# One tile's fp16 parts ahead of a normalisation, one weight's bound and split a group sooner, three products among the last contexts

## The reference

```python
xn = _layernorm(x, axis=-1)
q, k, v = (proj(Wq), proj(Wk), proj(Wv))            # xn @ W.T, 16 heads of 32
scores = einsum('bhqd,bhkd->bhqk', q, k) / sqrt(32)  # causal
ctx = einsum('bhqk,bhkd->bhqd', softmax(scores), v)
s = ctx @ Wo.T
hidden = fwht(silu(xn @ W1.T) * (xn @ W3.T))
out = x + s * silu(hidden @ W2.T)
```

## Time and profile before

| | us |
|---|---|
| median of 3 runs | 944.32 |
| lowest, highest | 943.84, 944.62 |
| the profiled execution | 944.66 |
| its span, first to last instruction | 943.0 |
| PE busy in the span | 928.3 (98%) |
| DVE, ACT, POOL busy | 728.0, 625.5, 339.0 |

### The profile page before, as it was taken

One profiled execution on the slowest core, in us unless ns is written; L12 is line 12 of the kernel. 1 busy time (PEld: TensorE's weight loads), 2 busy tenths in 40 slices (PEclk: granted clock), 3 DMA queues, 4 the chain that ended last, 5 costly groups with the idle time before them and its releaser, 6 DMA issues. The chain is left out here.

```text
span 943.0 us, 19017 instructions
## 1 busy us (share of the span) xinstructions
PE 928.3 (98%) x6500; PEld 566.6 (60%) x6500; DVE 728.0 (77%) x1416; ACT 625.5 (66%) x1340; POOL 339.0 (36%) x591
## 2 busy tenths in 40 slices
PE   8999999999999999999999999999999999999997
PEld 7764566666666656744468656566665666575443
DVE  7886998998998988846665579989898899833343
ACT  4456889989889877833344358787887888833221
POOL 1896664665665442000000114344344353410000
PEclk9999999999999999999999999999999999999999
DMA  9797245544343414661236622323323232150111
GB/s 291 270 252 228 80 114 151 143 118 118 86 121 90 118 31 124 221 226 44 67 103 244 201 57 80 91 58 95 76 75 92 61 81 58 46 202 22 45 45 45
DMA packets 57920, 110.09 MB, mean 117 GB/s; under 512 B 5600, under 2 KB 22624, under 8 KB 57312
## 3 DMA queue, kind: packets, MB, share of 16 engines
q1 hardware_dynamic: 57824, 108.88, 38.9%
HBM read 79.23 MB, written 29.36 MB: 115 GB/s over the span
## 5 line engine op out<-in xcount | busy, mean ns | idle before, releaser
L1264 DVE TENSOR_TENSOR p_lo<-stages,p_hi 128x512 f16<-128x512 f32 (+2 forms) x288 | 201.7, 710 | 25.3 <-ACT p_hi L878 23.7
L1613 PE MATMUL f<-x_hi,w_lo 128*128 128x512 f16 x512 | 195.6, 382 | 0.0
L1613 PE MATMUL f<-x_lo,w_hi 128*128 128x512 f16 x512 | 194.8, 380 | 0.0
L1613 PE MATMUL f<-x_hi,w_hi 128*128 128x512 f16 x512 | 194.5, 380 | 0.0
L868 ACT ACTIVATE stages<-s 128x512 f32<-128x512 f32 (+2 forms) x288 | 150.6, 524 | 57.9 <-PE s L1573 55.5
L878 ACT ACTIVATE p_hi<-stages 128x512 f16<-128x512 f32 (+2 forms) x288 | 160.5, 557 | 25.6 <-POOL stages L699 16.4
L1573 PE MATMUL s<-qk_st 98*128 98x512 f32 (+2 forms) x384 | 129.9, 416 | 1.7 <-DMA qk_st<-m_lo 1.5
L699 POOL TENSOR_SCALAR_AFFINE_SELECT stages<-stages 128x128 f32<-128x128 f32 x192 | 61.4, 325 | 167.9 <-ACT stages L868 167.4
L707 POOL TENSOR_TENSOR w_lo<-w,w_hi 128x256 f16<-128x256 f32 x128 | 95.5, 775 | 55.2 <-ACT w_hi L931 52.8
L1251 DVE CUSTOM_DVE_ANT_0 m<-m,causal 128x1024 f32<-128x1024 f32 (+1 forms) x98 | 104.5, 1066 | 3.8 <-PE m L1554 2.7
L986 ACT ACTIVATE h_hi<-hidden 128x1024 f16<-128x1024 f32 x32 | 33.8, 1057 | 97.1 <-PE f L1411 97.1
(11 more groups left out here) (224 smaller groups left out, 1907.9 us busy)
## 6 DMA issues: line engine op xcount, KB each, us to landing
qk_st<-qk_parts SPq DMA_DIRECT2D x96, 256.0 KB, 4.3
w<-w1w SPq DMA_DIRECT2D x32, 512.0 KB, 3.6
qk_parts<-qk_hi SPq DMA_DIRECT2D x32, 256.0 KB, 3.5
qk_parts<-qk_lo SPq DMA_DIRECT2D x32, 256.0 KB, 4.4
scan<-w1w SPq DMA_DIRECT2D x12, 512.0 KB, 5.6
wht_in<-w SPq DMA_DIRECT2D x4, 1024.0 KB, 10.6
w_butterflied<-wht_in SPq DMA_DIRECT2D x4, 1024.0 KB, 5.7
x_in<-x SPq DMA_DIRECT2D x16, 256.0 KB, 2.9
```

The costliest lines, as they stand in the source:

```text
L1264: dve.tensor_tensor(p_lo[s][:], expd[q % NE][:, 0:end - need], p_hi[s][:], ALU.subtract).then_inc(p_lo_done, 1)
L1613: mm = pe.matmul(F[m][:, 0, :], w, v, start=k == 0, stop=k == GMM - 1)
```

## The change

Three edits. In the projection of batch 0 the fp16 parts of tile 0 (`x16(b, 0)`) come ahead of the second normalisation, on ACT (the square root) and on DVE. The steps of Wv are each one group sooner: absolute values after groups 4 and 5, the bound after group 8, scaling after groups 9 and 10, splitting after groups 11 and 12 on DVE. (The scaling and splitting also in batch 1.) And in slot 194 the last three products of the network stand directly ahead of context 191.

```diff
-WV_ABS_AFTER = {5: (0, 1), 6: (2, 3)}
-BOUND_AFTER = 9
-WV_AT = {10: (0, 1), 11: (2, 3)}
+WV_ABS_AFTER = {4: (0, 1), 5: (2, 3)}
+BOUND_AFTER = 8
+WV_AT = {9: (0, 1), 10: (2, 3)}
+LAST_FFN = 3
...
@@ ACT, project
-                    if b == 0 and g == ROOT_AFTER:
-                        root(b, 1)
                     for t in XT_AFTER.get(g, ()):
                         xt(b, t)
...
                     for t in X16_AFTER.get(g, ()):
                         x16(b, t)
+                    if b == 0 and g == ROOT_AFTER:
+                        root(b, 1)
...
@@ DVE, project
-                    if b == 0 and g == ROOT_AFTER:
-                        normalise(b, 1)
                     for t in XT_AFTER.get(g, ()):
                         xt(b, t)
                     for t in X16_AFTER.get(g, ()):
                         x16(b, t)
                     if b == 0:
+                        if g == ROOT_AFTER:
+                            normalise(b, 1)
...
@@ PE, heads
                     kept = 1 if (g in CTX_PLAN or b == 0 and g in MAX_PLAN) and g < SLOTS else 0
+                    if g == SLOTS + 2:
+                        kept = LAST_FFN
                     some_ffn(at, ffn_upto(g) - kept)
...
                         for q in range(first, end):
+                            if q == SLOTS - 1:
+                                some_ffn(ffn_upto(g) - kept, ffn_upto(g))
                             context(n0 * NS + q)
...
-                    some_ffn(ffn_upto(g) - kept, ffn_upto(g))
+                    if g < SLOTS:
+                        some_ffn(ffn_upto(g) - kept, ffn_upto(g))
```

## The result

| | before | after |
|---|---|---|
| median, us | 944.43 (10 runs) | 948.93 (10 runs) |
| ratio, 95% interval | | 1.0047 (1.0034 to 1.0061) |
| the profiled execution, us | 944.66 | 950.89 |
| its span, us | 943.0 | 949.2 |
| TensorE busy in the span, us | 928.3 | 930.6 |

The change makes the kernel 4.5 us slower. The forecast was +1.7 (946.0, range 944.9 to 947.6), so the sign is right and the size is not. The ten executions after the change read like this, time and mean granted clock: 945.74 (0.999), 946.13 (0.999), 947.68 (0.996), 947.70 (0.998), 948.30 (0.995), 949.57 (0.996), 949.75 (0.996), 950.50 (0.996), 950.89 (0.995), 951.12 (0.995). The two in which the clock stayed at 0.999 took what was forecast.

A forecast was written before the change was run, and what follows sets the result against it. TensorE was taken as the bound, busy 928.3 of 943.0 us. Group 8 +2.58, V0 -0.91 and the rest 0 gave +1.7 us, so 946.0 against the median, with an 8-in-10 range of 944.9 to 947.6.

The forecast's parts named there:

- Tile 0's fp16 parts: Before tile 4's transpose: the 0.82 us wait goes, normalisation comes 0.60 later; the gain is worth nothing inside group 8's wait.
- The absolute values: Ahead of tile 7's lo part: four VectorE steps, in turns with GpSimd's additions, start group 8 2.58 us later.
- The tie at the third absolute value: VectorE and GpSimd start together there; VectorE was taken as served first, its step taking 0.68 us instead of 1.78.
- The slack of 0.27 us before group 8: Before the change, tile 7's lo part ended at 36.91 and group 8, which waits for it, started at 37.18.
- The bound, the split and V0: At the projection's end: with the Wv steps a group sooner, V0's wait goes, 0.91 us back.
- The last three products: End of each batch's heads: the wait only moves from context 191 to 190; worth 0, from -0.1 to +0.1 us.
- The clock: Rival: TensorE's clock falls to half in the wait before group 8, costing 1.5 us, 947.5; chance 0.10.
- The tie served to GpSimd: Rival: GpSimd goes first at the third absolute value, adding 1.10 us, 947.1; chance 0.20.
- "Faster": Rival: absolute values take plain 0.60 us slots without turns, group 8 starts at 37.0, 943.2 us; chance 0.07.

The follow-up runs named there:

- the run that priced it: Changed kernel with the absolute values on ScalarE, plus seven extra repeats of tile 7's lo part on VectorE: 949.20 us, 1.0059 to the kernel before.
- The kernel kept busy: Changed kernel with 24 extra identity transposes on TensorE ahead of its wait before group 8: 947.57 us, 1.0035 to the kernel before.
- the later slab load: Changed kernel with the 1 MB load of W2's second slab issued after group 1's stores: 946.21 us, 1.0022 to the kernel before.

## Why the prediction was wrong, step by step

- **Tile 0's fp16 parts: right.** The wait before tile 4 is gone, the normalisation and GpSimd's first addition are 0.60 later (GpSimd 27.59 against 26.46, where group 2's lo part, ahead of them, was already 0.53 later at 22.72), and the gain disappears in the wait before group 8. Alone it brings no gain that can be told.
- **The absolute values: the mechanism right, the size off.** From the end of `x16_lo(3)` to the end of `xt_lo(7)` the forecast had 39.64 - 31.39 = 8.25 us, the trace has 41.51 - 32.98 = 8.53. The tie at the third absolute value went to VectorE (0.68 us), as chosen, which is partly luck: in one of four traces it went the other way. The first was longer than thought (1.56 us; 32.64 - 31.39 = 1.25 in the forecast). What failed is the start of that chain. The prediction took 31.39 from the trace of before as a fixed time. It hangs on the landing of group 0's stores, which is no fixed time, and that trace had the earliest. The queue began 1.59 later, as ScalarE's step did (29.95 against 28.35), while TensorE was only 0.97 later by its start; the difference, 0.62, and the 0.28 of the chain are in the wait, which became 4.38 us instead of 3.5. The slack of 0.27 us before group 8 was of that trace as well: the trace of the last products alone, with the same order there, has 0.91 us of wait.
- **The bound, the split and V0: right.** V0 starts without a wait.
- **The last three products: right**, 1.0001 alone, and the wait moved from context 191 to 190.
- **The clock: here the prediction failed.** It put the fall at nothing in the sum and gave it a chance of 0.10 and 1.5 us, since "it holds through 4.5 us here". That number was one place of one trace, the end of the kernel. In the changed kernel it fell in at least 7 of 10 executions, and a fall cost 2.1 us in its trace, 2.3 in the run that priced it. The sum of the trace: forecast 1.67, the longer wait and the smaller V0 term (4.38 - 0.82 - 0.74 = 2.82 instead) + 1.15, the clock + 2.10, so +4.9; the medians differ by 4.5, and three of ten executions show no fall in their mean. The kernel kept busy gives about the same split: with the clock up the change costs 2.8 us instead of 1.7, and with its falls 4.5. So two steps failed, the wait (its fixed start time above all) by about 1.1 us and the clock by 1.7 to 2.1. The first alone gives some 947.1 and stays inside the range; with the clock the time lies outside.
- **The rivals.** The tie served to GpSimd didn't happen in the changed kernel's trace, but in that of the later slab load it did. The clock's fall did happen, and together with the wait it lies beyond the range. The Trainium skill (TensorE: Matmul & The Clock Gate, "Why this matters for your kernels") was cited for this rival; the runs agree with its warning of idle gaps between bursts: a 4.2 us wait cost 6.5 us. "Faster" would have needed absolute values of under 0.9 us on average; the runs have them only where GpSimd is quiet (1.28 for a pair) or on ScalarE.
- **ScalarE beside GpSimd.** The Trainium skill (SBUF — State Buffer, "Who interferes with whom") says that ScalarE never waits on anyone. The traces agree for this instruction: a pair of absolute values took 1.18 and 1.20 us on ScalarE beside GpSimd's additions, against 3.26 and 2.34 on VectorE.

What stays open: by what rule the clock falls 2.1 us into one wait, 1.5 us after the end of another, 0.3 and 0.5 us after waits of only 2.71 and 2.07 us, and not at all in one of 3.12 us. The traces show these cases and not what decides between them.

## What to carry to other kernels

Price a new wait of TensorE with the half pace that may follow it: here some 2 us on top, in a part of the executions of the kernels with 3 us, in 12 of 15 of the two with over 4, and behind waits of 2.71 and 2.07 us in one trace. A start time read from a trace is only as firm as what released it; where that is a DMA, take the spread of its landing into the range, since a chain with 0.3 us of slack turns it into a wait; one trace can be the luckiest, as it was here. And before a step is moved forward in a full queue, look for an idle engine: with the same four instructions on ScalarE the change gives 1.7 us, with them on VectorE it costs 4.5.

## What the runs showed of the hardware that I had not expected

- The clock can be halved after the wait is over: 1.5 us into resumed work at full pace, for 3.4 us (in the changed kernel it stayed halved for 6.8 us).
- 42 equal transposes at the start took 6.33 to 7.71 us from one execution to the next. Two traces have to be aligned behind them before they are compared.
- A store's issue occupied SyncE's queue for 4.8 us behind two loads of 1 MB, and for 0.33 us with one of them moved behind it.
- The clock fell behind waits of 2.71 and 2.07 us in one trace, and not behind one of 3.12 us in another.
